# A fused attention and expert layer on eight cores: zero-tile matmuls at the start, weights in quarters over six banks, one load of constants

## The reference, cut to what matters

```python
# x: (8, 2048, 1024), one sequence for each core; H = 8 heads of DK = 64
xn = layernorm(x)
q = elu(xn @ W_Q.T) + 1 ; k = elu(xn @ W_K.T) + 1 ; v = xn @ W_V.T
# for every head, over t:  S = gamma*S + k_t v_t^T ;  z = gamma*z + k_t
#                          y_t = (S^T q_t) / (z . q_t + 1e-6)
gate = sigmoid(xn @ W_g.T + b_g)
attn = (y * gate) @ W_O.T
# feed-forward: top 2 of 8 experts, softmax weights, rank-4 left/right factors
ffn  = xn @ W_lin.T + b_lin + sum_k w_k * ((xn . left[idx_k]) @ right[idx_k])
out  = x + attn + ffn
```

## Time and profile before

| | |
|---|---|
| time, median of 3 runs | 265.86 us (265.49 to 266.19) |
| the profiled execution's own time | 264.92 us |
| its span (slowest core, core 3) | 263.9 us; cores 262.6 to 263.9 us |
| mean granted clock of TensorE | 0.998 to 1.000 |
| busy: PE, DVE, ACT, POOL | 243.6, 162.8, 79.5, 61.7 us |
| chain that ended last | PE 84%, DVE 7%, issue 3%, DMA 3% |

### The profile page before, as it was taken

The page is one execution under the profiler, slowest core; times in us unless marked ns, Lnnn a source line. Parts: engine busy times, 40 slices in busy tenths (PEclk is TensorE's granted clock), DMA queues, the critical chain, the costliest instruction groups (busy, mean ns, idle before and its releaser), DMA issues.

```text
span 263.9 us, 5412 instructions; the slowest of 8 cores (262.6 to 263.9 us)
## 1 busy us (share of the span) xinstructions
PE 243.6 (92%) x1768; PEld 122.6 (46%) x1768; DVE 162.8 (62%) x425; ACT 79.5 (30%) x132; POOL 61.7 (23%) x99
## 2 busy tenths in 40 slices
...
GB/s 183 238 142 253 243 166 226 208 194 178 254 345 149 0 83 79 70 92 0 161 1 157 4 82 79 79 83 81 79 82 82 80 80 106 137 137 105 82 97 142
DMA packets 9615, 33.25 MB, mean 126 GB/s; under 512 B 1458, under 2 KB 1778, under 8 KB 9332
## 3 DMA queue, kind: packets, MB, share of 16 engines
...
## 4 chain that ended last, share of the span: by engine, by line
PE 84%; DVE 7%; issue 3%; DMA 3%; ACT 1%; SPq 0%; DVEq 0%; ACTq 0%
PE PJ L340 26%; PE L L362 17%; PE L L406 8%; PE PJ L333 7%; PE PJ L362 4%; PE L L340 4%; DMA x_sb<-x 3%; PE T L311 3%; PE L L333 2%; PE SY L354 2%; PE PJ L406 2%; PE T L347 2%; PE SY L378 1%; PE T L319 1%; PE T L392 1%
## 5 line engine op out<-in xcount | busy, mean ns | idle before, releaser
L362 PE MATMUL L<-wlin_sb,xnfm 128*128 128x512 bf16 x208 | 49.2, 379 | 0.0
L298 POOL TENSOR_SCALAR S_blk<-S_sb,small_s 128x260 bf16<-128x260 f32 x30 | 28.8, 973 | 85.8 <-DVE S_sb L775 85.6
L362 PEld LDWEIGHTS L<-wlin_sb,xnfm 128*128 128x128 bf16 x208 | 19.8, 98 | 23.2 <-issue 0.8
L844 ACT ACTIVATE e_sb<-PJ 128x512 bf16<-128x512 f32 x28 | 16.5, 593 | 42.1 <-PE PJ L340 40.6
L608 DVE TENSOR_SCALAR e_sb<-e_sb 128x512 bf16<-128x512 bf16 x32 | 9.4, 294 | 28.7 <-ACT e_sb L844 28.7
L820 ACT ACTIVATE xn_tm<-x_sb,nmr,rstd 128x1024 bf16<-128x1024 f32 x16 | 19.9, 1241 | 23.6 <-POOL nmr L254 22.1
L406 PE MATMUL L<-wo_sb,ygfm 128*128 128x512 bf16 x104 | 26.7, 379 | 0.0
L340 PE MATMUL PJ<-xnfm,wg_sb 128*128 128x512 bf16 x112 | 26.6, 379 | 0.0
L340 PE MATMUL PJ<-xnfm,wq_sb 128*128 128x512 bf16 x112 | 26.6, 380 | 0.0
L340 PE MATMUL PJ<-xnfm,wk_sb 128*128 128x512 bf16 x112 | 26.6, 380 | 0.0
L333 PE MATMUL PJ<-wv_sb,xnfm 128*128 128x512 bf16 x96 | 24.6, 400 | 0.0
...
## 6 DMA issues: line engine op xcount, KB each, us to landing
...
x_sb<-x POOLq DMA_DIRECT2D x6, 512.0 KB, 21.3
...
wv_sb<-wv POOLq DMA_DIRECT2D x4, 256.0 KB, 10.9
wq_sb<-wq POOLq DMA_DIRECT2D x2, 512.0 KB, 18.2
...
```

The lines of the kernel that those rows point to most:

```text
L298: GP.tensor_scalar(S_blk[:, :].rearrange("p (q w) -> p q w", q=4)[:, :, 65 * e : 65 * e + 65], S_sb[:, :].rearrange("p (q w) -> p q w", q= ...
L362: TE.matmul(lb(c, n)[:, :], xnk(k, c), wlin_sb[:, D * k + 512 * n : D * k + 512 * n + 512], start=False, stop=False)
L844: SE.activation(e_sb[:, 512 * (n % 2) : 512 * (n % 2) + 512], bank[:, :], AF.Exp).then_inc(ac_e, 1)
```

## The change

On SyncE the three loads of constants become one, `cst` (128 x 467 float32: mask pieces, small constants, and the identity packed in 64 columns), issued behind chunk 1. VectorE copies the identity and the small constants out of it, between the statistics of chunks 0 and 1. GpSimd issues the four V quarters as soon as VectorE's third `dv_ini` is there, without the wait for chunk 0, and loads W_Q, W_K and W_g in four quarters each. The 1/sqrt of chunks 1 and 3 moves from ScalarE to GpSimd (`rs(1)`, `rs(3)`), between its load issues. TensorE gets 22 matmuls of 128x128 by 128x512 on the zeroed `S_blk` ahead of the first transposition, 5 behind it and 2 inside the first V chunk; they write SY1, which nothing reads then. The ring has six banks (SY0 and SY1 too), and the order of the prologue on TensorE, VectorE and ScalarE is written anew.

```diff
+    cst = th_g[:, 0:467]
-    ring4 = [PJ[0], PJ[1], L[0], L[1]]
+    ring6 = [PJ[0], PJ[1], L[0], L[1], SYb[0], SYb[1]]
+    vb = [ring6[i] for i in (0, 1, 2, 3, 2, 1, 2, 1)]
+    qb = [ring6[i] for i in (4, 5, 0, 1)]
+    kb = [ring6[i] for i in (3, 4, 5, 0)]
+    gb = kb
...
         load_x(0)
         load_x(1)
-        SY.dma_start(ident[:, :], ident_d[:, :]).then_inc(d_id, 16)
+        SY.dma_start(cst, cst_d[:, :]).then_inc(d_cm, 16)
         load_x(2)
         load_x(3)
-        SY.dma_start(small[:, :], small_d[:, :]).then_inc(d_sm, 16)
-        SY.dma_start(cmat, cmat_d[:, :]).then_inc(d_cm, 16)
...
     def pool_program():
         GP.memset(mhalf[:, :], -0.5).then_inc(po_ini, 1)
-        GP.wait_ge(d_x[0], 16)
+        GP.wait_ge(po_ini, 1)
+        GP.wait_ge(dv_ini, 3)
         for i in range(4):
-            o = 2 * FH * i
-            GP.dma_start(wv_sb[:, o : o + 2 * FH], wv_d[:, o : o + 2 * FH]).then_inc(d_wv[i], 16)
-        wload_half(wq_sb, wq_d, 0, d_wq)
+            wload_q(wv_sb, wv_d, i, d_wv)
+        rs(1)
+        wload_q(wq_sb, wq_d, 0, d_wq)
+        wload_q(wq_sb, wq_d, 1, d_wq)
         xload(4)
+        rs(3)
...
+    def warm(n):
+        for _ in range(n):
+            TE.matmul(SYb[1][:, :], S_blk[:, 0:128], S_blk[:, 0:512], start=True, stop=True)
...
     def pe_program():
-        TE.wait_ge(d_id, 16)
+        TE.wait_ge(dv_z, 1)
+        warm(22)
+        TE.wait_ge(dv_id, 1)
         xtr(0)
+        warm(5)
         xtr(1)
         TE.wait_ge(dv_xev, 1)
+        TE.wait_ge(d_wv[0], 16)
+        vproj(0, vb[0], 0, 2)
+        warm(2)
...
+        for i in range(4):
+            TE.wait_ge(d_wq[i], 16)
+            for m in range(4):
+                if i == 0 and m >= 2:
+                    TE.wait_ge(ac_v, m - 1)
+                fproj(wq_sb, 0, m, qb[m], pe_q, 2 * i, 2 * i + 2)
         xtr(4)
+        TE.wait_ge(dv_xev, 5)
+        TE.wait_ge(ac_v, 4)
+        vproj(4, vb[4])
...
+        for i in range(4):
+            TE.wait_ge(d_wg[i], 16)
+            for m in range(4):
+                if i == 0:
+                    TE.wait_ge(dv_k, m + 1)
+                fproj(wg_sb, 0, m, gb[m], pe_g, 2 * i, 2 * i + 2)
+            if i == 0:
+                xtr(6)
+            if i == 1:
+                TE.wait_ge(dv_xev, 7)
+                TE.wait_ge(ac_v, 5)
+                vproj(6, vb[6])
         xtr(7)
...
         TE.wait_ge(d_lg, 16)
         tgp(0)
-        for c in (6, 7):
-            TE.wait_ge(dv_xev, c + 1)
-            TE.wait_ge(ac_g, c - 5)
-            vproj(c, L[c - 6])
+        TE.wait_ge(dv_xev, 8)
+        TE.wait_ge(ac_v, 6)
+        vproj(7, vb[7])
...
     def dve_program():
+        VE.memset(S_blk[:, :], 0.0).then_inc(dv_z, 1)
...
         stats(0)
+        VE.wait_ge(d_cm, 16)
+        VE.tensor_copy(ident[:, :], cst[:, 403:467].bitcast(BF16)).then_inc(dv_id, 1)
+        VE.tensor_copy(small[:, :], cst[:, 384:403]).then_inc(dv_sm, 1)
         stats(1)
         stats(2)
         xev_v(0)
         stats(3)
         xev_v(1)
```

194 lines of the change are left out of this document (91 added, 103 removed).

## The result

The changed kernel takes **271.42 us** (median of 4 runs, 269.88 to 271.58); the kernel before, on the same chip, 265.72 us (265.49 to 266.19). The ratio is 1.0193, with a 95% interval of 1.0166 to 1.0220: slower by 5.1 us (0.0193 of 265.7; the two medians are 5.7 us apart), where 1.2 were forecast. The profiled execution took 269.88 us; its slowest core is core 0, with a span of 268.7 us. It is the fastest and the mildest of the four: three of its cores have a mean clock of 0.987 or less, and in the other three executions five to seven have.

What follows compares the result with a forecast made beforehand. Bound taken: VectorE's work between the last transposed chunk and the first mask. Gains 4.3 us, losses 5.55, net +1.3: profiled 264.9 becomes 266.2; with the median 0.94 above it, 267.1 us, range 264.4 to 269.6.

Steps and rivals of the forecast that it cites:

- Q to chunk 7 transposed (start of `tgp`): TensorE's prologue after V of block 0, from Q through K and gate to chunk 7's transposition: 30.85 us, ending at 54.15.
- transposition and wait before V(4), V(5): On TensorE after Q and after K: 0.45 us to transpose the chunk, then 0.95 idle for its copy.
- waits in the first gate quarter: TensorE after V(5): 1.25 us idle, as gate tiles need `phi` of K, which VectorE delivers late.
- chunk 7 transposed to tg: VectorE's tail: copy of chunk 7, then `stats(8)`, no longer under gate matmuls; `tg_sb` at 56.5 instead of 55.24.
- the start: Prologue up to the end of V of block 0: 23.3 instead of 27.6 us, a gain of 4.3.
- if the faster step holds: Condition on the 4.3 us gain: zero matmuls keep V of block 0 at 0.216 us a matmul instead of 0.43.
- the rival with a chance of 0.22: TensorE's clock falls again in the gap before V(1), or is never lifted: slower, 269.3 or 269.9 us; chance 0.22.
- the floor rival: V ends at 21.3 to 22.2 if chunk 2 lands below 10.6 us: not slower, 265.6 us; chance 0.14.
- The order's 5.55 us: Loss from Q to `tg_sb` under the new order: 33.2 us where before it was 27.65.
- Quarters at no cost: Loading weights in quarters is slower, but gate weights land near 47.8, four microseconds ahead of need: cost nothing.
- Without that cover 1.9: Quarters' lower load rate over 3.1 MB would cost 1.9 us if gate weights were not ahead of need.
- The Trainium skill's rule on DMA: All DMAs share 16 engines, so earlier V weights swap places with chunks 2 and 3; last V quarter no sooner.

Runs made afterwards that it cites:

- e3: The changed kernel with more zero matmuls: 12 behind chunk 0's transposition, 6 behind chunk 1's, 4 inside V(0), for 5, 0 and 2; 269.48 us, ratio 1.0130.
- e4: The kernel before with only zero matmuls added, 22, 8 and 8 ahead of its first three transpositions; 263.51 us, ratio 0.9943.
- e13: The changed kernel's start, but the order and four banks of before from Q on, weights in halves, chunk loads at their old places; 266.91 us, ratio 1.0045.
- e14: The changed kernel with Q, K and gate weights loaded and waited for in halves instead of quarters; 270.27 us, ratio 1.0157.
- e12: e4 with Q, K and gate weights loaded in quarters, used in halves as before; 268.95 us, ratio 1.0109.
- e16: e13 with Q, K and gate weights in quarters instead of halves; 268.00 us, ratio 1.0068.
- e10: The changed kernel with the V weights issued behind the arrival of chunk 0 again; 271.04 us, ratio 1.0188.
- e7: e4 with the V weights issued behind the third `dv_ini`, without the wait for chunk 0; 266.41 us, ratio 1.0009.
- e8: e4 with one load of constants and its two copies on VectorE between the statistics of chunks 0 and 1; 264.19 us, ratio 0.9943.
- e18: e13 with the V weights issued behind the arrival of chunk 0 again; 266.06 us, ratio 1.0019.

## Why the prediction was right or wrong

**The sign was right, the size was not**: 1.2 us forecast, 5.1 us measured. Most steps behind V held:

| step | forecast | measured |
|---|---|---|
| Q to chunk 7 transposed (start of `tgp`) | 30.85 us | 30.96 on core 0, the same within 0.02 on every core |
| transposition and wait before V(4), V(5) | 1.40 | 1.66, 1.66 |
| waits in the first gate quarter | 1.25 | 0.9 |
| chunk 7 transposed to tg | 2.35 | 2.64 |
| tg to `av(0)` | 8.37 | 8.37 |
| idle before `av(0)` | 3 | 3.03 |
| last gate weights | 47.8 | 47.3 (core 0) |
| `cst` there | 8.0 | 8.1 |
| issue of the V weights | 3.6 | 4.13 |
| V of block 0 done, slowest core | 23.3 | 26.3 |
| `av(0)`, slowest core | 64.9 | 68.3 |

That 30.85 comes within 0.1 us is in part luck: twice 0.26 us too little ahead of V(4) and V(5) stands against 0.4 us too much in the gate quarter.

**The step that failed is the start.** The text took V of block 0 to end at 23.3, "if the faster step holds", and booked 4.3 us for it. On the slowest core it ends at 26.29: 1.3 us gained. Two things were mis-sized. The clock falls in the gap on three of the eight cores (0, 2 and 4) of the profiled execution, as the rival with a chance of 0.22 has it: its price was 2 to 2.5 us at the end of V, and 2.4 us lie between core 0 and core 6. Three cores are enough, since the slowest sets the time. The text had set against this rival that the trace shows no fall after a fast step; the trace of before could not show one, since TensorE has no fast step before the gap there. The Trainium skill (TensorE: Matmul & The Clock Gate, Part 1) has the slow clock as the default that activity lifts. The runs agree with it: 0.50 granted in the row of 15 to 20 us, and less time with more zero matmuls in e3. That rule was worth more than a chance of 0.22. Then, the V weights: the walk lets half of V(0) start at 13.9, behind the copy of chunk 0, and has no wait for the first quarter. It lands at 15.0 on core 0 and TensorE waits 1.58 us for it, in the very gap in which the clock falls. Chunk 2, which I took as the bound, is there by 10.1; the sign at which the floor rival was to hold came true, and V still did not end at 22.2. Core 6, which kept its clock, ends V at 23.93, so that of the 3.0 us by which 23.3 was missed 2.4 go with the clock and 0.6 with the later start of V. The rest of the distance from 267.1 to 271.42 is smaller: 0.3 us from chunk 7 to tg, and 1.5 us by which the median lies above the profiled execution, where the text took 0.94.

**The wrong core was the reference.** The 27.6 us of before belong to core 3, the latest; the other seven start Q at 25.3 to 26.6. Before, Q starts within 2.2 us over the cores and `av(0)` comes within 1.3: core 4, the earliest, takes 37.2 us between them and the latest 36.0. A late core does not catch up; an early one is held by what it waits for, as in e4, where Q starts within 1.9 us and `av(0)` within 0.6, behind waits for chunk 4. Where these waits are missing the old order doesn't even the cores out either (e13: Q within 4.8 us, `av(0)` within 4.6). The new order adds the same 41.98 us to every core, and so the time is the start of the worst of eight cores. The gain of the mean core is 1.6 us (26.4 to 24.8), and what it has to pay is 5.6.

**The order's 5.55 us** were right as read in the profiles (Q to tg is 33.60 instead of 27.66 on core 3 and 27.96 on five other cores; Q to `av(0)` 5.6 us less in e13 than in e14), and as a difference between kernels' times they are less: 3.0 us between e14 and e13, since there the four banks take a part back at the start of Q and the cores start further apart.

**Quarters at no cost** was right in sum for this kernel (some 1 us by e14, and the intervals allow none), for the reason given: the new order wants the gate weights late. "Without that cover 1.9" was low: 4.4 us in e12, since what comes late there is a chunk of x behind the last gate quarter too, which the text left out, and on core 0 the clock fell. In e16 the same swap is 0.6 us. Why it is so much less there isn't settled.

**The Trainium skill's rule on DMA** (DMA: Bandwidth & Descriptors, Issuing engines are not separate DMA queues) was weighed rightly: the V weights are issued 1.6 us sooner on the mean and land 0.6 to 0.7 us sooner, and e10 against the changed kernel shows no gain in time. The early issue costs, however, 0.66% on e4. The profiled execution of e7 shows how on one core: chunk 3 comes late, and the clock falls in the wait.

**The sum, by ratios of runs** (each a difference of two, good to some 0.3 or 0.4%; the steps lead from run to run, so that they add up whatever each is due to): zero matmuls -0.57% (e4); one constants load 0.00 (e8); new order of V, `rs` on GpSimd, fewer zero matmuls with the falls of the clock behind them, and the wait for V(0)'s copy +0.76 (e18 less e8, not told apart); V weights at once +0.26 (e13 less e18); order from Q on, with six banks and its places of the chunks' loads, +1.12 (e14 less e13); quarters +0.36 (the changed kernel less e14). Together +1.93%. Only the first is a gain, and without the others it stands. The third term and that of the order are clear of the noise; +0.26 and +0.36 are not.

**What stays open**: why the clock falls on some cores and not on others with nearly the same gap (core 6 waits 2.73 us ahead of chunk 1's transposition and keeps it; core 5 waits 1.42 us there and 1.68 us for the second V quarter, and keeps it); the size of the quarters' cost in e12 beside that in e16; and the changed kernel's start with zero matmuls ahead of each of its first three transpositions and the old order behind it, which no run has.
